# Row maxima of two heads in one VectorE instruction over two neighbouring PSUM banks, with banks given out by their places in the order

## The reference

```python
# x: (1, 2048, 128); 16 heads of 8; FFN width 352
xn = layernorm(x)
q, k, v = split(xn @ w_attn + b_attn)
scores = q @ k.T * 8 ** -0.5 + mask      # mask[i, j] = -log(j - i + 1) for j >= i, -inf for j < i
attn = softmax(scores) @ v @ w_proj + b_proj
# fp4: blocks of 16, scale = absmax / 6, values rounded to the E2M1 grid
h = silu(fp4(xn) @ fp4(w_gate).T) * (fp4(xn) @ fp4(w_up).T)
out = x + attn + fp4(h) @ fp4(w_down).T
```

## Time and profile before

| | |
|---|---|
| median of 3 runs | 763.8 us (759.39 to 765.53) |
| profiled execution | 762.22 us |
| its span, first to last instruction | 760.4 us |
| granted TensorE clock, mean | 0.903 |
| DVE maxima L940 | 640 instructions, 366.1 us |
| DVE weighings L967 | 198, 119.9 us |
| POOL weighings L638 | 221, 439.0 us |

### The profile page before, as it was taken

The page is one execution under the profiler, slowest core; times in us unless marked ns, Lnnn a source line. Parts: engine busy times, 40 slices in busy tenths (PEclk is TensorE's granted clock), DMA queues, the critical chain, the costliest instruction groups (busy, mean ns, idle before and its releaser), DMA issues.

```text
span 760.4 us, 11088 instructions
## 1 busy us (share of the span) xinstructions
PE 615.5 (81%) x3659; PEld 252.5 (33%) x3711; DVE 582.5 (77%) x1181; ACT 412.3 (54%) x881; POOL 551.3 (72%) x405
## 2 busy tenths in 40 slices
PE   4876395467978898989989799888889988889876
PEld 3333142313433242433324233232323323334332
DVE  7243133998878879798998988988899897878854
ACT  2333244223555565656565665656666676666674
POOL 7133010998878796988879789789789978868663
PEclk9557555566999999999999999999999999999999
DMA  5013400210001000000000100000000000000000
GB/s 153 16 31 81 114 37 15 63 30 1 1 20 45 2 0 1 2 1 15 2 0 22 43 1 2 16 0 2 2 1 1 2 2 0 2 15 2 2 2 15
DMA packets 13121, 14.44 MB, mean 19 GB/s; under 512 B 1441, under 2 KB 12722, under 8 KB 12722
## 3 DMA queue, kind: packets, MB, share of 16 engines
q1 hardware_dynamic: 12120, 13.35, 6.5%
q10 hardware_dynamic: 946, 0.40, 0.2%
HBM read 9.98 MB, written 3.42 MB: 18 GB/s over the span
## 4 chain that ended last, share of the span: by engine, by line
PE 45%; DVE 36%; issue 9%; ACT 5%; POOL 3%; ACTq 1%; DMA 1%; DVEq 0%
DVE mxp L940 16%; PE psum L1202 11%; PE psum L1155 9%; PE psum L1181 8%; DVE ring L967 6%; PE psum L1079 5%; POOL ring L638 2%; PE psum L1063 1%; PE psum L1116 1%; PE psum L1118 1%; DVE st L834 1%; PE psum L1184 1%; PE psum L1131 1%; ACTq L792 1%; PE psum L1158 1%
## 5 line engine op out<-in xcount | busy, mean ns | idle before, releaser
L638 POOL TENSOR_TENSOR ring<-ring,dist 128x1024 f32<-128x1024 f32 (+3 forms) x221 | 439.0, 2013 | 55.1 <-ACT ring L780 54.6
L940 DVE TENSOR_REDUCE mxp<-psum 128x1 f32<-128x512 f32 (+3 forms) x640 | 366.1, 605 | 136.1 <-PE psum L1158 95.1
L780 ACT ACTIVATE ring<-psum 128x512 f32<-128x512 f32 (+3 forms) x442 | 218.6, 532 | 195.0 <-PE psum L1184 100.0
L1155 PE MATMUL psum<-kop,qop 96*128 96x512 bf16 (+3 forms) x640 | 227.4, 372 | 56.4 <-DVE mxp L940 33.0
L1181 PE MATMUL psum<-qop,kop 128*128 128x512 bf16 (+3 forms) x588 | 201.6, 357 | 32.1 <-DVE mxp L940 14.0
L1202 PE MATMUL psum<-ring,vaug 128*32 128x512 f32 (+3 forms) x1280 | 152.7, 551 | 0.1
L1181 PEld LDWEIGHTS psum<-qop,kop 128*128 128x128 bf16 x640 | 62.4, 99 | 209.4 <-DVE mxp L940 76.5
L967 DVE TENSOR_TENSOR ring<-psum,dist 128x512 f32<-128x512 f32 (+3 forms) x198 | 119.9, 617 | 14.7 <-ACT psum L780 14.4
L780 ACT ACTIVATE psum<-psum 128x512 f32<-128x512 f32 (+3 forms) x198 | 99.6, 536 | 54.2 <-PE psum L1181 34.2
L1155 PEld LDWEIGHTS psum<-kop,qop 96*128 96x128 bf16 x640 | 64.9, 102 | 136.7 <-DVE mxp L940 70.5
L1184 PE MATMUL psum<-tri_k,identb 128*128 128x128 bf16 x256 | 54.8, 228 | 11.1 <-issue 10.8
(11 more groups left out here) (133 smaller groups left out, 540.1 us busy)
## 6 DMA issues: line engine op xcount, KB each, us to landing
kop<-parts_dram SPq DMA_DIRECT2D x9, 384.0 KB
qop<-parts_dram SPq DMA_DIRECT2D x9, 384.0 KB
parts_dram<-ring SPq DMA_DIRECT2D x18, 128.0 KB, 2.3
xin<-_attn_hidden_states_dram SPq DMA_DIRECT2D x4, 256.0 KB, 4.7
ring<-inv_dram SPq DMA_DIRECT2D x1, 1024.0 KB, 5.1
out_dram<-xin SPq DMA_DIRECT2D x4, 256.0 KB, 2.3
qop<-mrow ACTq DMA_DIRECT2D x48, 4.0 KB
wa<-in_L_attn_w_attn_dram ACTq DMA_DIRECT2D x1, 192.0 KB
```

The lines of the kernel that those rows point to most:

```text
L638: g_.tensor_tensor(slot(p)[:, :, 0:n], slot(p)[:, :, 0:n], both, ALU.mult).then_inc(weighed_pool, 1)
L780: a_.activation(scores if pair_vec[p] else slot(p)[:, e % 2, 0:n], scores, ACT.Exp, scale=SCALE).then_inc(exp_done, 1)
L940: v_.tensor_reduce(mxp[:, u % 2, 4 * a + j, c - g:c - g + 1], bank(*o)[:, 0:n], AX_X, ALU.max).then_inc(max_used, 1)
L1155: ins = mm(bank(*o)[:, 0:n], qop[0:K_MAX, u // NQ % 2, h, P * a:P * (a + 1)], kop[0:K_MAX, h, k0:k0 + n], start=True, stop=(c != g))
```

## The change

A maximum item is now `("max", u, a, j, c)` with j 0 or 2 and stands for heads j and j + 1. PE fills two banks b and b + 1, DVE reduces both in one instruction with two numbers a row. The 640 instructions become 320. Each half may have another last holder, for which PE waits separately. `flush` puts in two stages after each maximum item, ROWS_LATER counts 4 items, and each item costs the plan MAX_START = 150 ns.

The banks are now given out with a hard rule: `leaves[b]` is the place in the order of the item at which its holder's last reader stands, and only banks with `leaves[b] <= n` are open to an item at place n. A pair takes two neighbouring open banks with the least `held`; a gate takes bank 6 if it is open; others take the open bank whose end of use is least, among equals the one that leaves the most neighbouring couples.

```diff
@@ plan() @@
-            for j in range(4):
+            for j in (0, 2):
                 for c in range(g, NG):
-                    work = TPG - a if c == g else TPG
+                    work = 2 * (TPG - a if c == g else TPG)
...
-            vec_time += VEC_START + VEC_NS * P * work
+            vec_time += MAX_START + VEC_NS * P * work
...
         urgent.clear()
+        taken = 0
         while stages:
             item = stages.pop(0)
+            taken += 1
...
-            if not whole:
+            if not whole and taken == STAGES_AT_ONCE:
                 break
@@ build() @@
+    def left(o):
+        kind = o[0]
+        n = place[("gu", o[1]) if kind in ("gate", "up") else ("qk", o[1] // 2) if kind == "qp" else
+                  ("dist",) if kind == "dist" else o]
+        last = {"gate": "sum", "close": "norm", "project": "add"}.get(kind)
+        if kind == "st" and pair_vec[o[1] // 2]:
+            last = "weigh"
+        if kind == "qp":
+            return n, place[("qf", o[1] // 2)]
+        return n, place[(last, o[1])] if last else n
...
+    leaves = [-1] * BANKS
+    def pairs_without(taken, banks):
+        return sum(1 for b in banks if b + 1 in banks and taken not in (b, b + 1))
     for o in bank_items:
-        b = min(range(BANKS), key=lambda k: held[k])
-        bank_of[o], prior[o] = b, holder[b]
-        holder[b], held[b] = o, bank_held(o)
+        n, until = left(o)
+        open_banks = [b for b in range(BANKS) if leaves[b] <= n]
+        if o[0] == "max":
+            taken = min(([b, b + 1] for b in range(BANKS - 1) if b in open_banks and b + 1 in open_banks),
+                        key=lambda bs: (max(held[b] for b in bs), sum(held[b] for b in bs)))
+        elif o[0] == "gate" and GATE_BANK in open_banks:
+            taken = [GATE_BANK]
+        else:
+            taken = [min(open_banks, key=lambda b: (max(held[b], n), -pairs_without(b, open_banks), -b))]
+        for half, b in enumerate(taken):
+            bank_of[o + (half,) if o[0] == "max" else o] = b
+            prior[o + (half,) if o[0] == "max" else o] = holder[b]
+            holder[b], held[b], leaves[b] = o, bank_held(o), until
@@ DVE @@
-                    v_.tensor_reduce(mxp[:, u % 2, 4 * a + j, c - g:c - g + 1], bank(*o)[:, 0:n],
+                    v_.tensor_reduce(mxp[:, u % 2, 4 * a + j:4 * a + j + 2, c - g], two_banks(o)[:, :, 0:n],
                                      AX_X, ALU.max).then_inc(max_used, 1)
@@ PE @@
-                    bank_free(*o)
...
+                    for half in range(2):
+                        h = 4 * hq + j + half
...
+                        bank_free(*o, half)
+                        ins = mm(bank(*o, half)[:, 0:n], qop[0:K_MAX, u // NQ % 2, h, P * a:P * (a + 1)],
+                                 kop[0:K_MAX, h, k0:k0 + n], start=True, stop=(c != g))
+                        if c == g:
+                            ins = mm(bank(*o, half)[:, 0:P], identb[:], tri_q[:], start=False, stop=True)
                     ins.then_inc(scores_psum, 1)
```

More of the change, by code:

```diff
@@ L38 @@
 OUT_BANK = 7
+GATE_BANK = 6
 WARM = 30
@@ L54 @@
 SOON, SOON_MORE = 32, 24
-ROWS_LATER = 8
+ROWS_LATER = 4
 FFN_AT, FFN_GAP = 130, 122
-PARTS_STAGES, SILU_STAGES = 2, 9
-VEC_NS, VEC_START = 1.05, 70
+PARTS_STAGES, SILU_STAGES, STAGES_AT_ONCE = 2, 9, 2
+VEC_NS, VEC_START, MAX_START = 1.05, 70, 150
 POOL_NS, POOL_START = 1.95, 330
@@ L458, in bank, with two_banks @@
             return psum[:, bank_of[o], :]
+        def two_banks(o):
+            return psum[:, bank_of[o + (0,)]:bank_of[o + (1,)] + 1]
         def gate_of(i):
@@ L1135, in _ @@
                     g, hq, _ = parts_of(u)
-                    h = 4 * hq + j
                     m = max_no[o]
@@ L1139, in _ @@
                         pe.wait_ge(consts_ready, 6)
[L1140 to L1145, removed]
                     if g != GROUPS[0] and not seen_q[g]:
@@ L1151, in _ @@
                         pe.wait_ge(kop_loaded[c], 16 * 3)
-                    bank_free(*o)
                     k0 = P * (TPG * g + a) if c == g else GQ * c
                     n = GQ * (c + 1) - k0
[L1155 to L1158, removed]
+                    for half in range(2):
+                        h = 4 * hq + j + half
+                        if g == GROUPS[0] and a == 0:
+                            if u == 0:
+                                pe.wait_ge(sel_vec_done, sel_vec.index(("sel", 0, h)) + 1)
+                            else:
+                                pe.wait_ge(sel_act_done, sel_act.index(("sel", 0, h)) + 1)
+                            pe.wait_ge(sel_act_done, sel_act.index(("sel", 1, h)) + 1)
+                        bank_free(*o, half)
[3 more added lines that the diff above has]
+                            ins = mm(bank(*o, half)[:, 0:P], identb[:], tri_q[:], start=False, stop=True)
                     ins.then_inc(scores_psum, 1)
```

## The result

The changed kernel takes 869.2 us (median of 4 runs, 869.14 to 874.23) against 764.7 us of the kernel before (4 runs): a ratio of 1.142, 95% interval 1.137 to 1.146. The direction was forecast; the size was not (785, range 748 to 815). The profiled execution has a span of 867.4 us against 760.4.

A forecast was written before the change was run, and what follows sets the result against it. DVE's row of instructions was taken to set the pace most of the time, PE refilling banks as DVE frees them. 762.2 - 18.4 + 71.3 - 38 + 7.0 = 784.1 us, about 785 for the median; range 748 to 815.

The forecast's parts named there:

- The pair instruction: DVE's maxima, units 4 to 15: one reading over two banks saves 0.064 us of start, 288 times, 18.4 us.
- Rivals 2, 3 and 5: DVE's pair readings: whole 0.149 start saved, 760 us, 0.05; two starts, 802; instruction splits, above 830; latter two together 0.12.
- Not all of it shows: DVE before maxima, units 4 to 15: of 71.3 us new holes, 38 fall in 65.2 already idle.
- Rival 1: DVE before pair maxima, 200 to 720 us: all 65.2 us of old idle time swallows holes; 756.9 or 750; chance 0.22.
- What such a handover costs: DVE waiting for a bank just released: 0.78 us if both banks hang on that release, 0.56 if only the second.
- both banks concerned: Units 4 to 15: 51 pairs with no DVE work between release and use, at 0.78 us each, 39.8 us.
- Rival 4: PE's queue, units 4 to 15: `st` waits on pair readings, POOL and ACT starve; 19 us more, 803; chance 0.15.
- Stages two at a time: DVE's FFN stages: 64 couples in direct sequence, each 0.11 us for the dependence, 7.0 us; ends 0 and 64 x 0.15.
- The rest: ROWS_LATER, MAX_START, GATE_BANK, PE's matmuls and clock: no shift of work between DVE and POOL, nothing added to the time.
- The clock: PE's granted clock could fall if PE stands more; taken at nothing.

The follow-up runs named there:

- 837: The changed kernel with one stage ahead of each pair and one behind it in place of two behind it; 836.6 us.
- 930: The changed kernel with pairs taking turns between banks 0-1 and 2-3, all others preferring 4 to 6; 929.9 us.

## Why the prediction was wrong, step by step

The ladder from the kernel before to the changed one, each step between two runs (most of them single, so that a step is uncertain by some 8 us):

| step | us | forecast |
|---|---|---|
| order in pairs, ROWS_LATER, MAX_START (762 to 778) | +15 | 0 |
| stages two at a time (778 to 802) | +25 | +7.0 |
| bank rule with two neighbours (802 to 828) | +25 | with the next: +33 (71.3 - 38) |
| joint handover (828 to 887) | +60 | |
| one instruction for two readings (887 to 869) | -18.3 | -18.4 |

The forecast missed by 85 us (784.1 to 869.2). Of these, 52 are the banks and the handover (85 measured, 33 forecast), 18 the stages, 15 the order. A slip in the prediction's own working is small: with 48 swallowed and nothing for the stages its sum gives 767, not 772, as the lower end of the forecast's own range.

**The pair instruction: right.** 320 readings over 2 x 512 columns and less; one follows the other's start after 1.14 us (509.77 to 510.91), as the sum from 0.536 a head and one start of 0.064 said. The form's mean, to be laid beside the earlier trace rows:

```profile
L975 DVE TENSOR_REDUCE mxp<-psum 128x2 f32<-128x1024 f32 x224 | 273.7, 1223 | 151.7 <-PE psum L1191 116.6 <-PE psum L1194 33.1
```

Recorded 1223 ns, as 149 + 1024 x 1.047 = 1221 gives. The rule of the Trainium skill ("VectorE: DVE Perf Modes", "The DRAIN you can't avoid") taken by itself would have made the gain 0.149 a pair, 42.9 us; the 18.3 us of the run with two readings speak for 0.064. The same section adds that an operation that isn't held starts earlier, and the 0.60 us from start to start agree with that. Rivals 2, 3 and 5 are out.

**"Not all of it shows" is the step that failed first.** I took 38 us off the 71.3 because DVE already stood 65.2 us before maxima. The idle time there was forecast at 98 us from 200 to 720 us and measured 139.4; over the whole span it grew by 100 us. Rival 1 is dead. But this step alone doesn't carry the miss: with nothing swallowed the sum is 822 us, 47 short of 869. Nor do the runs show how much of the old holes lies within the new ones. What the rows show is that the new holes are longer than a release and two matmuls, since PE, once let go, still has `st` and `pv` in front of the pair (521.70 to 530.74 at full clock, 511.05 to 515.58 with the slow clock in it).

**"What such a handover costs" was mis-sized.** 0.78 us a place is release, two matmuls, signal. Those are the pieces of a PE that has nothing else to do. (Of the 51 places called "both banks concerned", the bank loop has 28 with both and 23 with the first bank only; the second matmul stands behind the first, so the price is the same.) The bank rule and the joint handover measured 25 + 60 = 85 us against 71.3 before and 33 after the deduction. What was missing, as I read the rows, is the queue: I walked DVE's row only and asked what DVE had to do between release and use. PE's row is in order too, and the wait at its head holds `st` and `pv` that have free banks. The count gave 74, 73 and 19 us for kernels that take 869, 837 and 930: it ranks them wrongly, though it falls where only the estimates changed (76 places to 30) and the time fell by 36. Rival 4 named this queue, but priced it at 19 us. Its sign came: POOL waited 97.8 us for ACT from 200 to 720 us, where over 65 was to speak for it. No run isolates what the queue costs.

**"Stages two at a time" was priced by the wrong thing.** I took the dependence, 0.11 a couple, and it is there (508.18 to 508.74 is 0.56, a packed one 0.44). Its 7 us are the small part in the order in pairs. The two stages with their weighing are 1.59 us of DVE's row ahead of the next reading (508.18 to 509.77), and PE's head waits for it. The runs say 10 to 13 us in the kernel before, 25 in the order in pairs, up to 33 in the changed one.

**"The rest" was not nothing.** The order in pairs is about 15 us. It rests on a single run and includes the plan's changed costs. Its idle time stands before DVE's weighings, not before the maxima, so the two `st` in a row, whose exp and weighing come later, are a likely place; no run shows it.

**The clock** was taken at nothing and wasn't (below). Of the idle time before the maxima of units 4 to 15, the waits that ended at the lower clock are 26 with 31.7 us, before 3 with 1.5; those that ended at the full clock are 156 with 143.8 us, before 95 with 65.5. So most of the growth stands at full clock. No run isolates the clock.

**What stays open.** How much of each step is the lower clock, how much the queue behind PE's head costs by itself, what of the old holes lies in the new ones, and which part of the 33 us for stages on both sides is the earlier `sum` and `norm`.

## What to carry to other kernels

Before two instructions on a shared buffer are joined, price the handover, not the instruction: here 0.064 us of start was bought with a wait for the second matmul and a longer hold of the first bank, 60 us for 18. Where two in-order engines refill and drain the same few banks, walk both rows against each other, with all that stands behind a waiting instruction; here a count from one side ranked variants wrongly. And the estimates by which banks and fillers are placed can be worth more than the instruction: one constant (10 to 6) and a stage ahead of the maximum gave 3% on the kernel before.

## What the runs showed of the hardware that was not expected

A VectorE reduction over two neighbouring PSUM banks costs nothing extra at the crossing: 1223 ns recorded for 1024 columns, on the same line as 685 for 512; over 2 x 256 columns it was 688.

TensorE's granted clock was lower in the kernel in which PE waits more. Granted clock from 200 to 720 us: 0.99 before, 0.93 now, with PE busy 454 and 397 us of the 520. In units 4 to 15 it was at the lower of its two levels (1.2 GHz, shown as 0.50) for 104.6 us, before 35.3. In the stretch shown, PE is busy in about half of 508 to 512 us and the clock then is at that level until 515.4, in which eight `pv` matmuls take 1.94 us in place of 1.07. Columns are the stretch, its length, PE's busy time, the clock:

```profile
506.00:508.00 2.00, 1.79 (x12) 1.00 0.00 0
508.00:510.00 2.00, 1.03 (x7) 1.00 0.00 0
510.00:512.00 2.00, 0.95 (x6) 1.00 0.00 0
512.00:514.00 2.00, 2.00 (x9) 0.50 0.00 0
514.00:516.00 2.00, 2.00 (x11) 0.65 0.00 0
516.00:518.00 2.00, 0.77 (x4) 1.00 0.00 0
```

Another lull, 602 to 606 us with PE busy 1.74 of 4, left the clock where it was:

```profile
602.00:604.00 2.00, 1.20 (x8) 1.00 0.01 4
604.00:606.00 2.00, 0.54 (x6) 1.00 0.00 0
606.00:608.00 2.00, 2.00 (x22) 1.00 0.00 0
```

So a hole on PE can cost twice, itself and slow matmuls behind it, but need not. Over the span PE's busy time rose from 615 to 642 us for the same matmuls.
